# Two heads' units of the first attention group among the last chunk's projection products, and seven visits of value products per group

## The reference, cut to what matters

```python
B, S, C, H, D, E = 4, 2048, 512, 16, 32, 8
xn = layernorm(x)                                  # no gain, no bias
qkv = xn @ qkv_w.T + qkv_b                         # q, k, v of 16 heads
attn = softmax(q @ k.T * D ** -0.5)                # per batch and head, 2048 x 2048
a = (attn @ v).reshape(B, S, C) @ proj_w.T + proj_b
idx = top2(xn[:, 0, :] @ Wr + br)                  # two of 8 experts per batch
h = gelu(xn @ W1[idx] + b1[idx])
f = sum over the two of (h @ W2[idx] + b2[idx]) / 2
out = x + a + f
```

## Time and profile before

| | us |
|---|---|
| median of 3 runs | 4660.69 |
| lowest, highest | 4658.37, 4661.96 |
| the profiled execution | 4660.65 |
| its span, first to last instruction | 4658.9 |

### The profile page before, as it was taken

How to read it: one execution, slowest core, us unless ns; L and a number is a source line. 1 busy time by engine, 2 the same in 40 slices (tenths; PEclk the granted TensorE clock), 3 DMA queues, 4 the chain that set the end, 5 groups by cost and what they waited for, 6 DMA issues and landing times.

```text
span 4658.9 us, 65600 instructions
## 1 busy us (share of the span) xinstructions
PE 4623.1 (99%) x24396; PEld 2958.7 (64%) x24396; DVE 3206.6 (69%) x5313; ACT 2392.8 (51%) x4649; POOL 3176.1 (68%) x1105
## 2 busy tenths in 40 slices
PE   8999999999999999999999999999999999999999
PEld 7888888888755555555555555555555555555567
DVE  5233233333388888888888888888888888888854
ACT  2112121121146666666666666666666666666631
POOL 1121212121268999999999999999999999999910
PEclk9999999999999999999999999999999999999999
DMA  5334353434346666566666666665666666666557
GB/s 176 108 118 138 95 163 93 133 117 135 104 100 135 131 138 135 130 136 135 132 139 133 132 136 134 136 135 128 138 137 132 135 135 132 138 133 136 120 181 259
DMA packets 263425, 629.23 MB, mean 135 GB/s; under 512 B 46788, under 2 KB 83652, under 8 KB 224712
## 3 DMA queue, kind: packets, MB, share of 16 engines
q0 software_dynamic: 36288, 264.26, 27.9%
q1 hardware_dynamic: 226824, 360.85, 27.5%
HBM read 224.96 MB, written 134.74 MB: 77 GB/s over the span
## 4 chain that ended last, share of the span: by engine, by line
PE 62%; POOL 5%; DMA 3%; issue 2%; ACT 1%; DVE 0%; POOLq 0%; DVEq 0%
PE st_ps L1493 20%; PE o_ps L1419 18%; PE mx_ps L1407 18%; POOL p_pair L1121 4%; PE mx_ps L1433 3%; PE st_ps L1441 3%; DMA p_pair<-p_pair 3%; PE mx_ps L1441 1%; ACT p_sb L1197 1%; POOL p_pair L1159 0%; PE mx_ps L1412 0%; POOL o_inv L1115 0%; POOL p_pair L1125 0%; ACT front L1207 0%; DVE y_in L1286 0%
## 5 line engine op out<-in xcount | busy, mean ns | idle before, releaser
L1232 DVE TENSOR_REDUCE unit_max<-mx_ps 128x1 f32<-128x512 f32 x4016 | 2456.4, 682 | 311.1 <-PE mx_ps L1407 309.0
L1197 ACT ACTIVATE p_sb<-st_ps 128x512 f32<-128x512 f32 x4096 | 2063.3, 628 | 860.4 <-PE st_ps L1493 860.3
L1121 POOL TENSOR_TENSOR p_pair<-p_sb 128x2048 f32<-128x2048 f32 x504 | 2433.5, 4875 | 6.7 <-PE mx_ps L1433 3.4
L1419 PE MATMUL o_ps<-p_sb,v_sb 128*32 128x512 f32 x8192 | 986.7, 599 | 0.0
L358 POOL TENSOR_TENSOR h_lo<-h_f,h_hi 128x512 fp32r<-128x512 f32 x128 | 165.3, 1291 | 709.1 <-DVE h_hi L576 709.1
L1419 PEld LDWEIGHTS o_ps<-p_sb,v_sb 128*32 128x32 f32 x8192 | 214.1, 109 | 433.9 <-issue 286.2
L426 ACT ACTIVATE h_f<-rot,b_sb 128x512 f32<-128x512 f32 x128 | 88.1, 689 | 656.0 <-PE rot L627 655.9
L1493 PE MATMUL st_ps<-q_x,k_x 97*128 97x512 f32 x1024 | 401.0, 413 | 1.8 <-ACT p_sb L1197 1.4
L1493 PE MATMUL st_ps<-front 97*128 97x512 f32 x1024 | 399.3, 410 | 1.1 <-ACT p_sb L1197 1.1
L1493 PE MATMUL st_ps<-q_x,front 97*128 97x512 f32 x1024 | 399.1, 410 | 0.0
L1493 PE MATMUL st_ps<-front,k_x 97*128 97x512 f32 x1024 | 398.6, 410 | 0.0
(11 more groups left out here) (124 smaller groups left out, 5922.2 us busy)
## 6 DMA issues: line engine op xcount, KB each, us to landing
p_pair<-p_pair POOLq DMA_DIRECT2D x252, 1024.0 KB, 7.6
xt<-x SPq DMA_DIRECT2D x64, 256.0 KB, 2.7
stage<-w SPq DMA_DIRECT2D x32, 512.0 KB, 4.2
q_hi_d<-qk_hi SPq DMA_DIRECT2D x64, 256.0 KB, 3.1
q_lo_d<-qk_lo SPq DMA_DIRECT2D x64, 256.0 KB, 3.6
k_hi_d<-qk_hi SPq DMA_DIRECT2D x64, 256.0 KB, 2.7
k_lo_d<-qk_lo SPq DMA_DIRECT2D x64, 256.0 KB, 3.4
v_d<-v_out SPq DMA_DIRECT2D x64, 256.0 KB, 2.3
```

The costliest lines, as they stand in the source:

```text
L1121: pool.tensor_tensor(p_pair[:, slot, :, :], p_sb[:, n % SLOTS, :, :], p_sb[:, (n + 1) % SLOTS, :, :], ALU.add).then_inc(pair_done, 1)
L1197: act.activation(p_sb[:, (L * G * KT + n) % SLOTS, h, :], st_ps[bank(g, m)][:, :], ACT.Exp, scale=SCALE).then_inc(exp_done, 1)
L1232: dve.reduce_max(unit_max[:, n // 4, n % 4:n % 4 + 1], mx_ps[UNIT_PLACE[n] % RING][:, :], AX.X).then_inc(bank_read, 1)
L1419: op = pe.matmul(o_ps[rows, :], v_sb[u][:, kt, rows], p_sb[:, (L * G * KT + n) % SLOTS, h, :], start=(kt == 0), stop=(kt == KT - 1))
```

## The change

1. 32 units (heads 0 and 1 of group 0) move from the hidden part of the last chunk into its projection products: `UNITS_OF` puts none in the first two, four in each of the next six, two in each of the four value products (`with_units`). They use the four `acc` banks (`unit_bank`). Their queries and keys are loaded by `load_early` into the free half of `xnT_lo` and `xnT_hi` and, for head 1, into the place of `xt`; SP issues these nine DMAs ahead of the last chunk's first q/k stores.
2. The hidden steps 3 to 7 hold eight units each, not twelve, and the last holds eight, not four, which takes in the 16 of the second group; nothing is left behind the last output product. The row maxima are reduced after step 6 (`TURN_AT`) and transposed ahead of the last output products.
3. `STEPS` 4 has no visit, and the one of `STEPS` 5 handles four key tiles (6 to 9). Behind it a unit stands before the first score.

```diff
+                def load_early():
...
+                    for part, src in enumerate((qh_d, ql_d, qh_d)):
+                        sp.dma_start(early_q[part * D:(part + 1) * D, :, :].bitcast(F32),
+                                     src[0, :, 0:TOK].rearrange("(h d) n -> d h n", d=D)).then_inc(early_ld[2], 16)
+                    for h in range(EARLY_HEADS):
+                        for part, src in enumerate((kh_d, kh_d, kl_d)):
+                            sp.dma_start(early_k[h][part * D:(part + 1) * D, :].bitcast(F32), src[0, h * D:(h + 1) * D, :]).then_inc(early_ld[h], 16)
...
-        UNITS = [(0, 0)] * 3 + [(4, 8)] * 5 + [(0, 4)]
+        UNITS_OF = [0] * 2 + [4] * 6 + [2] * 4
+        UNITS = [(0, 0)] * 3 + [(2, 6)] * 5 + [(0, 8)]
+        TURN_AT = 8
...
+                        if last and i == NCH - 1:
+                            load_early()
                         for m in range(8):
...
-                    if n < 2:
-                        pe.wait_ge(v_done, B * NCH * TT - 1 + n)
+                    if n < 4:
+                        pe.wait_ge(y_added, B * NCH * TT - 2 * TT + n + 1)
+                    elif early:
+                        pe.wait_ge(front.bank_read, n - 3)
...
+                def with_units(out, pairs, u):
+                    n = sum(UNITS_OF[:u])
+                    for c in range(CC):
+                        op = split_product(out, pairs[c:c + 1], c == 0, c == CC - 1)
+                        if c < CC - 1:
+                            for k in range(UNITS_OF[u] * c // CC, UNITS_OF[u] * (c + 1) // CC):
+                                unit(n + k)
...
-                 "USUSUSUVSSUSUUSUS", "USUSUSUVSSUSUUSUS", "USUSUSUVTSSUSUUSUS", "USUSUSUVZSSUSUUSUS"]
+                 "USUSUSUSUSUSUSUS", "USUSUSUVUSSUUSUSS", "USUSUSUVTSSUSUUSUS", "USUSUSUVZSSUSUUSUS"]
...
-                            for kt in (2 * j - 2, 2 * j - 1):
+                            for kt in range(2 * j - (2 if "V" in STEPS[j - 1] else 4), 2 * j):
```

More of the change, by code:

```diff
@@ L117, in dense_stage @@
         acc = [ctx.enter_context(nc.psum_tensor(f"acc{i}", [P, 512], F32)) for i in range(TT)]
+        early_ld = [sem(f"early_ld{i}") for i in range(3)]
         const_ld, x0_ld, row_ld, zeroed = (sem(n) for n in ("const_ld", "x0_ld", "row_ld", "zeroed"))
@@ L554, in turn @@
                                 expert_lo(b, LATE_M[m])
+                            if last and i == NCH - 1:
+                                units(sum(UNITS_OF[:m]), UNITS_OF[m])
                             if not (last and i == NCH - 1):
@@ L568, in turn @@
                             dve.tensor_tensor(v_out[:, t % 2, :], rot[t % 4][:, :], v_bias[:, :], ALU.add).then_inc(v_done, 1)
+                            if last and i == NCH - 1:
+                                units(sum(UNITS_OF[:8 + t]), UNITS_OF[8 + t])
                         end = last and i == NCH - 1
@@ L595, in turn @@
                             if end:
[L596 to L601, removed]
+                                units(first_unit(8) + UNITS[8][1] // TT * t, UNITS[8][1] // TT)
                 for b in range(B):
@@ L684, in last_hidden @@
                                     unit(n + m)
[L685 to L691 removed]
+                    for h in range(4):
+                        pe.wait_ge(front.head_ld[h], 48)
                 def turn(b, last):
@@ L705, in turn @@
                             cols = slice(m * P, (m + 1) * P)
-                            split_product(rot[u % 4][:, :], [((wq_hi[:, c, cols], wq_lo[:, c, cols]), (xnT_hi[:, s, c, :], xnT_lo[:, s, c, :]))
-                                                             for c in range(CC)], True, True).then_inc(ready["qk"], 1)
+                            pairs = [((wq_hi[:, c, cols], wq_lo[:, c, cols]), (xnT_hi[:, s, c, :], xnT_lo[:, s, c, :])) for c in range(CC)]
+                            if last and i == NCH - 1:
+                                with_units(rot[u % 4][:, :], pairs, u).then_inc(ready["qk"], 1)
+                            else:
+                                split_product(rot[u % 4][:, :], pairs, True, True).then_inc(ready["qk"], 1)
                             u += 1
@@ L713, in turn @@
                             rows = slice(t * P, (t + 1) * P)
-                            split_product(rot[u % 4][:, :], [((xnT_hi[:, s, c, rows], xnT_lo[:, s, c, rows]), (wq_hi[:, c, 2 * C:], wq_lo[:, c, 2 * C:]))
-                                                             for c in range(CC)], True, True).then_inc(ready["v"], 1)
+                            pairs = [((xnT_hi[:, s, c, rows], xnT_lo[:, s, c, rows]), (wq_hi[:, c, 2 * C:], wq_lo[:, c, 2 * C:])) for c in range(CC)]
+                            if last and i == NCH - 1:
+                                with_units(rot[u % 4][:, :], pairs, u).then_inc(ready["v"], 1)
+                            else:
+                                split_product(rot[u % 4][:, :], pairs, True, True).then_inc(ready["v"], 1)
                             u += 1
```

63 lines of the change are left out of this document (44 added, 19 removed).

## The result

| | median, us | ratio to before, 95% interval | profiled execution: span, us |
|---|---|---|---|
| before | 4661.3 (4 runs beside it) | | 4658.9 |
| after | 4717.7 (4715.7 to 4721.2) | 1.0122 [1.0108, 1.0136] | 4713.9 |

The account below looks back on a forecast made before the run. TensorE, 99% busy, was taken to set each group's 49.2 us by its own slots and visits. Forecast: 4660.65 + 50 (longer groups) - 3 (less disturbance) + 14 (dense stage) = 4722 us, range 4697 to 4747.

Parts of the forecast that it names:

- The ring of four banks: Merged visit: each unit waits for the read four units earlier, reads 0.60 us apart; 12.35 us against 11.64, +0.71 a group.
- rival A: Attention: each removed visit gives back 0.34 us, 22 in all; with the dense term 4653 us; chance 0.05.
- The unit first behind the visit: Stretch behind the merged visit: exponentials start 0.23 us later, the eighth score waits; 4.05 us in place of 3.96, +0.09.
- The sum of a group: Attention: a group becomes 0.80 us longer, in 63 of 64 groups, +50 us.
- The disturbance: Attention: 0.2 us a group beyond the undisturbed 49.2; more slack for GpSimd removes some, -3 us.
- C with 0.90 us a group: High end of the range: rival C together with groups 0.90 us longer, given as 4747 us.
- The wait for the early loads: Last chunk's projection products: TensorE waits 11.8 us at unit 0, until queries and head 0 land at 1223.5.
- The second stall: Projection product 3: unit 4 waits for the read of unit 0 behind displaced stores and ScalarE's late copy, 4 us more.
- The chain of each product: Later projection products: first unit waits for ScalarE, VectorE's split and read; 1.5 us for four products, 0.8 once in value products.
- What came back: Dense end: the hidden steps, with 40 units in place of 60, give back 7 us, and the tail 9 us.
- rival C: Projection products: the wait drops TensorE's clock to 0.50 and recurring stalls keep it down, 8 to 17 us, 4730 to 4739; chance 0.12.
- the late eighth unit: Attention before the change: a stretch's last unit has its weights loaded after 0.20 us of waiting for VectorE.

Follow-up runs that it names:

- Half reads: Kernel before with each attention unit read over 256 of 512 columns, exponentials at an eighth of the scale: 4646.4 us with eight visits, 4643.1 with seven.
- experiments 1 and 5: Kernel before with the merged visit (seven a group), no early units: 4704.3 us; the same with units read over 256 of 512 columns, exponential scale an eighth: 4643.1 us.
- experiment 3: Kernel before with the merged visit, no early units, but a score in place of a unit first behind the merged visit: 4698.5 us.
- experiment 2: Changed kernel with the eight visits of before, so only the early units are left: 4675.6 us against 4660.5, ratio 1.0033.
- Experiment 9: Early units alone with loads issued in the chunk before; then VectorE's unit reads moved ahead of its split: 4660.7 us, ratio 1.0000 to before.
- experiment 6: Kernel before, eight visits, no early units, scores and units alternating behind each visit: 4650.6 us against 4660.5, ratio 0.9977.
- experiment 11: Early units with loads sooner, second head's loads behind product 1's stores, reads ahead of splits, plus alternating order, eight visits: 4644.7 us, ratio 0.9965 to before.

## Why the prediction was right

**Which part costs what.** Foreseen were 47 us for the attention and 14 for the dense end. Alone they measured 42.5 and 15.1; in the trace of after they are 39.5 and 15.3 (15.5 at the first copy).

**The ring of four banks.** Foreseen was 8.75 us from the first score to the merged visit; with 1.86 us of visit and 0.86 of sums in front that is 11.47 from visit to visit, and 11.47 is the median. The units wait as foreseen: each adds 0.13 us to TensorE's own pace (0.60 against 0.47), and the reads stand 15 in a row. Half reads take 1.03 us off it. This was the step on which the sign hung, and it was right for the reason given: rival A fell with experiments 1 and 5.

**The unit first behind the visit.** Foreseen +0.09 us a group; the new waits of scores for ScalarE are there (67.9 us), and experiment 3 gives 0.07.

**The sum of a group.** Foreseen +0.80, measured 49.94 against 49.21 in neighbouring undisturbed groups, +0.73. The 0.07 too much are in two places: the stretch behind the merged visit came out at 7.61 and not 1.86 + 1.74 + 4.05 = 7.65, and the three old stretches are 0.01 us longer each than I had them (5.83 in place of 5.82, and 6.69 with the sums in place of 6.68). The disturbance fell by 6.5 us and not 3 (63 x 0.73 = 46.0 against the measured 39.5): 2.3 of it in the last group, which took 53.85 us and now takes 52.24 where 0.73 more would have been due, the rest in small pieces: four groups of before are 0.6 to 0.9 us over their median, and in the trace of after none but the last is more than 0.5 off. That GpSimd's slack does this, as I had it, no run tests. The upper bound of my range doesn't follow from its terms either: C with 0.90 us a group adds up to 4745, not 4747.

**The wait for the early loads.** Foreseen 11.8 us, measured 11.93; loads from 1213.70 where I had 1212.3, landing of the first head at 1225.0 (11.3 us after the first issue, foreseen 11.2). TensorE was later by the 1.2 us by which the whole chunk started later in this execution (1206.7; among the traces of the variants with early units this start lies between 1204.9 and 1207.1, so it is no effect of the edit).

**The second stall.** Foreseen 4 us at full clock with the slower passes hidden under it; measured was 1.2 us from one pass to the next in place of 0.23, and the passes before it at half clock took the rest, 14 of them 0.43 us in place of 0.23 (2.8 us). The sum, 3.9, is right; its division was not, so in part this is luck. The nine issues took 5.8 us on SP and not 4.3, but the stores landed at 1228.65 and 1229.68 (foreseen near 1229), since they queue behind the loads. By then the product itself was the later one: ScalarE's copy started at 1230.62, released by TensorE. It was a near thing: in experiment 2 the copy started at 1230.32, released by the store.

**The chain of each product.** Foreseen 1.5 us for four products and 0.8 once; measured from pass to pass 1.63 to 1.71 in place of 0.23, four times, and 0.94 once: 1.4 and 0.7. Experiment 9 shows the mechanism, since the reads ahead of the split take these away.

**What came back.** The hidden products begin at 1270.64, 31.8 us later than at 1238.86 before, or 30.6 without the later start (foreseen 30). From there to the first output addition it is 53.2 us in place of 61.4: -8.2 (foreseen -7). From that addition to attention's first product:

```profile
1323.88 0.68 DVE L633 TENSOR_TENSOR y_out<-acc,x_res 128x512 f32<-128x512 f32 x1
...
1328.24 0.69 DVE L633 TENSOR_TENSOR y_out<-acc,x_res 128x512 f32<-128x512 f32 x1 [0.69 <-DMA y_d<-y_out]
1330.04 0.69 DVE L633 TENSOR_TENSOR y_out<-acc,x_res 128x512 f32<-128x512 f32 x1
...
1335.92 0.76 PE L1467 MATMUL mx_ps<-front 96*128 96x512 f32 x1 [5.09 <-PEq L211]
```

12.0 us in place of 20.3: -8.3 (foreseen -9), with the third and fourth addition 4.4 and 6.2 us behind the first (foreseen 4.7 and 6.5).

**The clock, rival C.** It did not stay down: half speed from 1217.7 to 1231.4, and 1.00 through all the stalls of 1.6 us behind it. At attention's start it was at 0.50 as before, but for 10.2 us (1330.4 to 1340.6) in place of 20.5, which the prediction had left out. It is worth little: behind attention's first product 4.7 us are left of it, where it was 5.9, and before that product TensorE stood for 5.09 us anyway.

**Where my reading failed** was in the experiments, not in the forecast: I took the late eighth unit for a cost of 1.1 us a group that a better order could bring back. It is 0.2 us a group (49.24 to 49.05). And I took GpSimd for what limits every group, which no run bears out. Waits at weight loads that end just before the next visit do not add up one to one; only those in a row do, since each of them moves the next.

## What to carry to other kernels

A pause of one engine may be the time in which a slower consumer catches up. Before removing it, write down the pace of the consumer (0.60 us) beside that of the producer (0.47) and count how many items fit into the ring between two pauses: eight did (the last of them 0.03 us late in effect), sixteen did not. Where loads are moved ahead on an in-order queue, the price is not only when they land but everything behind them; moving the loads put a residual's load and an output store behind them, and easing those left a product's store. Filling a stage's idle engine with work from elsewhere needs the other engines' queues in the right order as much as it needs the operands.

## What the runs showed of the hardware

A reduce of 128x512 out of PSUM takes 682 ns, one of 128x256 takes 423: 256 columns are worth 0.26 us, so by these two 0.16 us of a read don't depend on the columns. Ahead of a visit, a unit whose weights go in late is followed by the visit's weights after 0.43 us, an unhindered one after 0.55 (2005.96 to 2006.51 in experiment 6), so a short lateness is mostly absorbed there. Nine loads issued within 5.8 us on one queue landed between 1218.1 and 1228.2, about 1.3 us apart. And the granted clock was at 0.50 inside the attention (4135 to 4138) behind one wait of 2.3 us of TensorE (experiment 11), where it was at 1.00 from 4120 to 4131 and again from 4139.
